# Attention with two 64-row matmuls side by side in the TensorE array, and its normalisation and weight casts on VectorE

## What is computed

```python
qkv = hidden @ qkv_w.T + qkv_b                # 16*64 + 2*4*64 columns
xq, xk, xv = split(qkv)                       # 16, 4 and 4 heads of 64
xq = xq * scale                               # scale from softplus(scaling)
scores = einsum('bqhd,bkhd->bhqk', xq, xk)    # keys repeated for 4 query heads each
probs = softmax(scores, axis=-1)              # over 4096 keys
out = einsum('bhqk,bkhd->bqhd', probs, xv) @ o_w.T + o_b
x = layernorm(x + out)
x = layernorm(x + routed_experts(x) + shared_expert(x))
```

## Time and profile before

| what | value |
|---|---|
| median of 2 timed runs | 6644.26 us (6531.06 and 6757.47) |
| the profiled execution | 6530.7 us |
| its span, slowest core (of 6509.0 to 6529.3) | 6529.3 us |
| PE busy | 4877.2 us, 75% |
| ACT busy | 2690.2 us, 41% |
| DVE busy | 2400.5 us, 37% |
| first exponential to last `x1t` tile | 487.5 to 4005.9 us |

### The profile page before, as it was taken

The page is one execution under the profiler, slowest core; times in us unless marked ns, Lnnn a source line. Parts: engine busy times, 40 slices in busy tenths (PEclk is TensorE's granted clock), DMA queues, the critical chain, the costliest instruction groups (busy, mean ns, idle before and its releaser), DMA issues. The chain is left out here.

```text
span 6529.3 us, 83801 instructions; the slowest of 8 cores (6509.0 to 6529.3 us)
## 1 busy us (share of the span) xinstructions
PE 4877.2 (75%) x26053; PEld 2625.3 (40%) x26244; DVE 2400.5 (37%) x4956; ACT 2690.2 (41%) x2603; POOL 0.5 (0%) x5
## 2 busy tenths in 40 slices
PE   4867777767777677777677775699489938993997
PEld 2322222222222222222222221488258826881786
DVE  2323333343333433334333335344534353444444
ACT  1117777656777577775677761000000000010011
POOL 0000000000000000000000000000000000000000
PEclk9778888888888888888888886799689958995998
DMA  2111011120000211001111003012201211111111
GB/s 71 52 51 30 30 30 31 38 71 30 30 30 30 71 36 33 30 30 53 48 32 37 23 1 116 20 78 79 90 35 64 98 71 40 78 78 71 59 68 56
DMA packets 92642, 329.58 MB, mean 50 GB/s; under 512 B 12225, under 2 KB 12225, under 8 KB 75714
## 3 DMA queue, kind: packets, MB, share of 16 engines
q1 hardware_dynamic: 92226, 324.22, 14.5%
HBM read 259.04 MB, written 65.01 MB: 50 GB/s over the span
## 5 line engine op out<-in xcount | busy, mean ns | idle before, releaser
L589 ACT ACTIVATE pb<-psS,consts 128x1024 bf16<-128x1024 f32 x2048 | 2222.7, 1111 | 775.5 <-PE psS L550 755.8
L570 PE MATMUL psC<-pb,Vp 128*65 128x512 bf16 x4096 | 1352.4, 414 | 482.5 <-ACT pb L589 388.6
L570 PEld LDWEIGHTS psC<-pb,Vp 128*65 128x65 bf16 x4096 | 340.6, 116 | 1482.4 <-issue 1481.4
L919 ACT ACTIVATE gs<-psS 128x1024 bf16<-128x1024 f32 x160 | 163.7, 1023 | 1676.3 <-PE psS L897 1676.2
L550 PE MATMUL psS<-QT,padE 128*128 128x512 bf16 x1978 | 651.7, 414 | 213.8 <-DVE padE L517 210.2
L550 PE MATMUL psS<-QT,padO 128*128 128x512 bf16 x1955 | 643.0, 412 | 134.2 <-DVE padO L517 125.1
L897 PE MATMUL psS<-x1f,ew 128*128 128x256 bf16 x5120 | 597.8, 276 | 23.3 <-DVE gu L931 19.4
L949 PE MATMUL psC<-gu,ew 128*128 128x256 bf16 x5120 | 589.7, 274 | 10.4 <-DVE y_acc L968 10.4
L905 PE MATMUL psS<-x1f,ew 128*128 128x256 bf16 x5120 | 585.1, 273 | 0.0
L517 DVE COPY padO<-KTC 64x128 bf16<-64x128 bf16 x1024 | 195.0, 190 | 1035.6 <-PE psS L550 1022.0
L517 DVE COPY padE<-KTC 64x128 bf16<-64x128 bf16 x1024 | 193.1, 189 | 1036.6 <-PE psS L550 1022.9
(11 more groups left out here) (115 smaller groups left out, 2253.5 us busy)
## 6 DMA issues: line engine op xcount, KB each, us to landing
ew<-ewb SPq DMA_DIRECT2D x129, 1024.0 KB, 7.8
ewb<-ewcast SPq DMA_DIRECT2D x120, 256.0 KB, 3.2
x0b<-x SPq DMA_DIRECT2D x32, 512.0 KB, 3.5
cstage<-wg SPq DMA_DIRECT2D x32, 512.0 KB, 4.4
cstage<-wu SPq DMA_DIRECT2D x32, 512.0 KB, 4.2
cstage<-wd SPq DMA_DIRECT2D x32, 512.0 KB, 3.9
x0r<-x SPq DMA_DIRECT2D x32, 512.0 KB, 3.5
x1s<-x1t SPq DMA_DIRECT2D x32, 512.0 KB, 2.7
```

The source lines that it names most:

```text
L570: ins = tn.matmul(psC[0:65, R + m * 512:R + m * 512 + w], Vp[g][:, 65 * k2: 65 * k2 + 65], pb[k2 % 2][:, m * 512:m * 512 + w], start=st, s ...
L589: SC.inc(sc.activation(pb[kt % 2][:, 0:QC], pst[:, 0:QC], AF.Exp, bias=consts[:, CNC:CNC + 1]))
L919: b.S(lambda p_=p_, n=ic_n * TS: sc.activation(gs[p_][:, 0:n], psA[:, 0:n], AF.Silu))
```

## The change

Attention takes two query heads at a time. The number of queries in a chunk, `QC`, goes from 1024 to 512, so there are 8 chunks, each with 8 pairs of heads and 32 key tiles.

- The host reorders the query heads (`_head_perm`), so that the two heads of a `QT` tile belong to the two key heads of a `KTC` tile. The pad tiles and their copies go. The scores of the two heads are two matmuls of 64 rows each, at array positions (0, 0) and (64, 0), straight from `KTC`, into two banks of `psS`. The exponential is still 128x1024: two heads by 512 queries.
- `Vp` has 128 columns for each key tile: 64 of values and 64 of ones, the ones first for odd value heads. The value product of a head is split into the lower and the upper 64 keys, again at (0, 0) and (64, 0), each summed in a bank of its own. Four matmuls a step, four banks: all of `psC`, with no second half for the next pair.
- `emit_fin` takes the place of `emit_evac`: eight DVE operations on 64x512 add the halves of values and sums (which now stand on 64 partitions, so the broadcast matmul goes), then two reciprocals and two multiplications. It is issued at the second step of the next pair. The first values of the next pair wait for the eight.
- The casts of the expert weights go from ACT to DVE, two after each pair, in the queue ahead of that pair's `emit_fin`.
- The `soft_barrier` at the start of a chunk goes; an output part now has 4 tiles of 128 tokens.
- The cast of the output weights is issued before the cast helpers are defined; the scratch row in `x0r` and the wait for it go.

```diff
-                QC=1024, TCW=512, TC=1024, TS=256)
+                QC=512, TCW=512, TC=1024, TS=256)
...
-    Vp = [_a(nc.sbuf_tensor(f"Vp{g}", [128, 65 * kt_n], BF16)) for g in range(G)]
+    Vp = [_a(nc.sbuf_tensor(f"Vp{g}", [128, 128 * kt_n], BF16)) for g in range(G)]
...
-        b.V(lambda g=g: vc.memset(Vp[g][:], 0.0))
-        b.V(lambda g=g: vc.memset(
-            _ap2(Vp[g], 64, [[65, kt_n]]), 1.0))
+        b.V(lambda g=g: vc.memset(Vp[g][:], 1.0))
...
-                                Vp[g][:, 65 * kt: 65 * kt + 64],
+                            vdo = 128 * kt + (64 if g % 2 else 0)
+                            b.V(lambda g=g, vdo=vdo, co=co: vc.tensor_copy(
+                                Vp[g][:, vdo:vdo + 64],
...
-        for _t in padE + padO:
-            b.V(lambda _t=_t: vc.memset(_t[:], 0.0))
...
-            EWI[sl].wait(sc, (i // 2 + 1) * 16)
-            EWO.wait(sc)
-            b.S(lambda sl=sl, n=cpc * ncols: sc.activation(
-                ewcast[:, 0:n], cstage[sl][:, 0:n], AF.Identity))
-            b._cast_sc[sl] = SC.n
-            SC.wait(sy, b._cast_sc[sl])
+            EWI[sl].wait(vc, (i // 2 + 1) * 16)
+            EWO.wait(vc)
+            b.V(lambda sl=sl, n=cpc * ncols: vc.tensor_copy(
+                ewcast[:, 0:n], cstage[sl][:, 0:n]))
+            b._cast_vc[sl] = VC.n
+            VC.wait(sy, b._cast_vc[sl])
...
+        def emit_fin(st):
+            p, pvlast, first_of_qc = st
+            TN.wait(vc, pvlast)
+            if first_of_qc:
+                TN.wait(vc, b._oproj_tn)
+            b.V(lambda: vc.tensor_copy(mrgP[0:64, :], psC[0:64, 0:QC]))
+            b.V(lambda: vc.tensor_add(mrgP[0:64, :], mrgP[0:64, :],
+                                      psC[0:64, 512:512 + QC]))
...
+            b.V(lambda: vc.tensor_copy(mrgS[0:64, :], psC[0:64, 1024:1024 + QC]))
+            b.V(lambda: vc.tensor_add(mrgS[0:64, :], mrgS[0:64, :],
+                                      psC[0:64, 1536:1536 + QC]))
             b._psC_free_v = VC.n
...
+            b.V(lambda: vc.reciprocal(mrgR[0:64, :], mrgS[64:128, :]))
+            b.V(lambda: vc.reciprocal(mrgR[64:128, :], mrgS[0:64, :]))
+            b.V(lambda p=p: vc.tensor_tensor(
+                attnF[p][0:64, :], mrgP[0:64, :], mrgR[0:64, :], ALU.mult))
+            b.V(lambda p=p: vc.tensor_tensor(
+                attnF[p][64:128, :], mrgP[64:128, :], mrgR[64:128, :], ALU.mult))
+            b._attn_div_v = VC.n
...
-            b.soft_barrier()
...
+            for p in range(nQ):
+                kc = p // rep
+                gE, gO = 2 * kc, 2 * kc + 1
...
+                        SC.wait(tn, b._expslot.get(sl, 0))
+                        if p == 0 and kt < 2:
+                            VC.wait(tn, oslot_free.get(("ps", sl), 0))
+                        tn.matmul(psS[0:128, so:so + QC],
+                                  KTC[kc][0:64, ko:ko + 128],
+                                  QT[p][0:64, q0:q0 + QC],
+                                  start=True, stop=True, tile_position=(0, 0))
+                        TN.inc(tn.matmul(psS[0:128, so + QC:so + 2 * QC],
+                                         KTC[kc][64:128, ko:ko + 128],
+                                         QT[p][64:128, q0:q0 + QC],
+                                         start=True, stop=True,
+                                         tile_position=(64, 0)))
...
+                        tn.matmul(psC[0:128, 0:QC], Vp[gE][0:64, vo:vo + 128],
+                                  pb[slp][0:64, 0:QC], start=st, stop=sp,
+                                  tile_position=(0, 0))
+                        tn.matmul(psC[0:128, 512:512 + QC],
+                                  Vp[gE][64:128, vo:vo + 128],
+                                  pb[slp][64:128, 0:QC], start=st, stop=sp,
+                                  tile_position=(64, 0))
+                        tn.matmul(psC[0:128, 1024:1024 + QC],
+                                  Vp[gO][0:64, vo:vo + 128],
+                                  pb[slp][0:64, QC:2 * QC], start=st, stop=sp,
+                                  tile_position=(0, 0))
+                        TN.inc(tn.matmul(psC[0:128, 1536:1536 + QC],
+                                         Vp[gO][64:128, vo:vo + 128],
+                                         pb[slp][64:128, QC:2 * QC], start=st,
+                                         stop=sp, tile_position=(64, 0)))
                         pv_val[k2] = TN.n
-                        expbuf_free[k2 % 2] = TN.n
-                    if kt == kt_n - 1 and h + 1 < H:
-                        hn = h + 1
-                        gn = hn // rep
-                        padsn = padO if hn % 2 else padE
-                        rowsn = slice(64, 128) if hn % 2 else slice(0, 64)
-                        emit_pad_copy(hn, 0, padsn, rowsn, gn // 2, gn % 2)
-                        emit_pad_copy(hn, 1, padsn, rowsn, gn // 2, gn % 2)
+                        b._pbslot[slp] = TN.n
...
+                        TN.wait(sc, b._pbslot.get(sl, 0))
+                        SC.inc(sc.activation(pb[sl][:, 0:2 * QC],
+                                             psS[:, sl * 1024:sl * 1024 + 2 * QC],
                                              AF.Exp, bias=consts[:, CNC:CNC + 1]))
                         exp_val[kt] = SC.n
-                        sbuf_free[sl] = SC.n
-                pending_evac = (h, p, odd, R, Rn, dict(pv_val))
-
+                        b._expslot[sl] = SC.n
+                pending_fin = (p, pv_val[kt_n - 1], p == 0)
...
-                if sq == 0:
-                    TN.wait(sy, getattr(b, "_bcast_tn", 0))
...
+def _head_perm(H=16, KVH=4, Dh=64):
+    rep = H // KVH
+    qperm = []
+    for p in range(H // 2):
+        e = 2 * (p // rep) * rep + p % rep
+        qperm += [e, e + rep]
+    rows = []
+    for h in qperm:
+        rows += list(range(Dh * h, Dh * h + Dh))
+    return qperm, np.array(rows)
```

More of the change, by code:

```diff
@@ L513, in emit_pad_copy @@
[L513 to L520 removed]
+        b._expslot = {}
+        b._pbslot = {}
+        b._psC_free_v = 0
+        b._oproj_tn = 0
+        b._attn_div_v = 0
+        b._x1st = {}
@@ L544, in build_program @@
                         sl = kt % 2
-                        pst = psA if sl == 0 else psB
-                        SC.wait(tn, sbuf_free.get(sl, 0))
-                        VC.wait(tn, copy_val[(h % 2, kt)])
-                        for m in range(nqmm):
-                            w = min(512, QC - m * 512)
-                            ins = tn.matmul(pst[:, m * 512:m * 512 + w],
-                                            pads[sl][:, :],
-                                            QT[p][:, q0 + m * 512: q0 + m * 512 + w],
-                                            start=True, stop=True)
@@ L672, in build_program @@
         X0R[0].wait(sy)
+        X0R[1].wait(sy)
         WS[0].wait(sy)
@@ L676, in build_program @@
         EWO.wait(sy)
-        WR.wait(sy)
     nc.all_engine_barrier()
```

158 lines of the change are left out of this document (48 added, 110 removed).

## The result

The changed kernel is faster: it took 6057 to 6067 us, the kernel before 6527 to 6534; the ratio is 0.9265 (95% interval 0.9222 to 0.9308). "After" is a second profiled execution of the changed kernel (6055.99 us, cores of 6030.4 to 6054.9).

The account below looks back on a forecast made before the run. Bound: latency through TensorE, ScalarE 16% below. Steps 2335, boundaries 454, chunk ends 368 and cold first steps 10 make 3167 us against 3518: −351, start +3, from 6530.7 to 6183 us; range 6040 to 6320.

Parts of the forecast that it names:

- step: Attention's steady loop through ScalarE and TensorE: 1.14 us a step instead of 1.22, with 0.05 us of stagger; −160 us.
- boundary: Between groups of heads: first values wait for eight VectorE operations, 8.1 us lost instead of 12.1; −270 us over all.
- chunk end: Last normalisation, output projection and layer norm of a chunk: 46 us, eight ends instead of four of 71; +85 us.
- start: Before the first exponential: filling `Vp` +7 us, less small strided fills, their gaps and the pad fills: +3 us.
- R1: Score and value pairs of each step queue: 1.44 us a step, 6945 us, +6.3%; chance 0.12.
- R2: In each step's pairs, a weight load waits for the matmul on its own rows: 1.265 us, 6465, −1.0%; chance 0.08.
- R3: TensorE granted its lower clock throughout: 1.49 us a step, 6830 us; half of the time, 6505; chance 0.07.
- The pad copies: 2048 copies of 0.19 us leave VectorE: hidden in steady steps, worth nothing; at boundaries they were the 4.59 us wait.
- The casts: 120 expert-weight casts of 0.69 us move from ScalarE to VectorE, running in mid-group with nobody waiting behind.
- The cover: For the casts in mid-group: VectorE's other work there is 6.3, 6.9, 1.6 and 1.4 us in a 44 us group.

## Why the prediction was right, point by point

The sum of 3167 us for attention stands against 3072.3 measured on core 0; by its terms, with the 29 us of the start:

| term | forecast | measured | worked out |
|---|---|---|---|
| step | 1.14 | 1.117 | 2048 × −0.023 = −47 |
| boundary | 8.1 | 7.4 | 56 × −0.7 = −39 |
| chunk end | 46 | 45.2 | 8 × −0.8 = −6 |
| start | +3 | −29 | −32 |
| sum of the differences | | | −124 |

6183 − 124 = 6059, against 6056 measured. That it fits to 3 us is in part luck: the terms are those of core 0, whose span went from 6529.3 to 6046.0 us, while the 6056 go by core 5 (6054.9), the slowest one after.

- **The step** was right in its mechanism. The second of a pair starts 0.00 to 0.02 us behind the first where I had taken 0.05, so the step is at the end of its own range (1.115). The Trainium skill's few nanoseconds (TensorE: Matmul & The Clock Gate, Part 3) were nearer than my estimate.
- **R1, R2.** Neither came, as the pairs show. R1's price was mis-sized: on equal rows the kernel took some 8870 us, not 6945, since its 2.87 for a two was reckoned at the full clock and 5.12 was measured. Its place and sign were right; I priced it at the full clock, and no row showed what clock such a stream gets.
- **R3, the clock,** did not come either, and yet it is the rival that was nearest to the truth of the kernel. I argued against it that TensorE would be streaming 86% of a step. That argument is wrong: two experiments had TensorE streaming all of the time at 0.50. What saved the forecast is that the halves of the array worked side by side. The chance of 0.07 was too low for what I knew.
- **The pad copies** I called hidden and worth nothing in the steps. Their time was hidden, but the zero rows were not nothing: without them, and without pairs, the kernel takes 17% more, most of it by the lower clock and some by the changes of height. A change in two parts (pads out first, pairs later) would have looked like a failure at its first part.
- **The casts** were costed at nothing, and cost nothing. The cover named for it was right: VectorE has time in mid-group. "Without the cover they would be in front of the eight copies" could not be seen here; in the kernel before, where the casts fall ahead of the normalisation, the move costs 72 us.
- **The boundary** follows the working: the third exponential at 8.91 for 9.2, eight operations of 0.69, one long gap of 5.67 us, no idle time on ScalarE for a store of `ewb`. Only the clock's part was too dear: the seven steps from the third exponential on take 8.29 us on average instead of 7.82, so 0.5 is lost where I had 1.2. Taken as here, from third exponential to third exponential, a boundary before costs 50.89 − 32 × 1.22 = 11.8 us; my 12.1, from cast to cast, was 0.3 too much.
- **The chunk end** is right to 1 us, with the 5.57 us after the last activation for "about 5". The working named two causes for the 10.7 us taken off there, fewer tiles and no barrier, and didn't part them: with the barrier put back it is 2 us, so the tiles are the cause of the rest.
- **The start** is the step that failed. I took the removed barrier for a matter of the chunk ends and the moved output weights for a line that changes place. At the first chunk the barrier waited for VectorE to finish eight loads and casts of output weights, 31 us from the first cast to the last and 37 from the end of the last `Vp` copy, that nobody needs before the first chunk's end. The row was in the prediction's own groups: 487.49 with 41.73 us of idle time ahead of it. The other half, filling `Vp`, was too cheap: one fill takes 3.47 us where 3.5 was expected, but the first cast of the projection's weights starts 7.4 us later than before (38.54 against 31.14) and the last `Vp` copy ends 8.2 us later (457.2 against 449.0), so the 4 us of small fills and gaps that I took off were not there to be taken. The two together: 8.2 later, and the first exponential 1.0 after the last `Vp` copy instead of 38.5, make the 29 us.

Three errors of one sign (steps, boundaries, start) make nearly all of the 127 us between 6183 and the measured time; none of them is large by itself.

## What to carry to other kernels

Two products of 64 rows gain by standing on different halves of the array in the same stretch of time; one at a time they were worth less here than products padded with zeros, since the clock stayed at its lower level and each change of height cost time as well. When a barrier or a wait is removed, work out what it held at the first pass too, and look at the idle time ahead of the stage's first instruction. Join small VectorE operations on half the partitions into one over all, and split an accumulation in two only if its banks have a spare set, since it must be drained before the next group can begin. Look at where an operation will fall in the queue that takes it up: the same casts fell in mid-group in one kernel and at the boundary in the other.

## What the runs showed of the hardware that I had not expected

- TensorE at 1.2 GHz without a gap: granted clock 0.50 for 64-row products one after another (matmuls 0.43 us apart, TensorE busy 30.00 of 30 us) and for single 64-row scores between 128-row values; 1.00 for zero-padded 128-row ones and for 64-row pairs side by side, also between 128-row values.
- A matmul on free rows starts ahead of an earlier one in the program (1504.96 against 1505.17).
- A change between 128-row and 64-row products costs about 0.10 us at the full clock (0.31 between starts instead of 0.21) and 0.13 at the lower one (0.56 instead of 0.43), both ways.
- VectorE needs 0.69 us for 64x512 and for 128x512 out of PSUM.
